# A graph kernel: the last weight's turning moved from the second aggregation into node tiles 4 to 7 of the first linear

## The reference

```python
def sage(h, W_self, W_neigh, b):           # mean over incoming edges
    agg = segment_sum(h[src], dst, num_segments=N)
    return h @ W_self + (agg * deg_inv[:, None]) @ W_neigh + b

h = relu(sage(x, W_self0, W_neigh0, b0))
x = layernorm(x + sage(h, W_self1, W_neigh1, b1))
# second layer, self loops added, norm = deg^-1/2 of both ends
g = einsum('nd,od->no', x, W) + b          # W is used turned: W[o, d]
out = segment_sum(norm[:, None] * g[col], row, num_segments=N)
x = layernorm(x + out)
```

## Time and profile before

| | |
|---|---|
| median of 3 runs | 849.19 us (848.74 to 851.98) |
| the profiled execution's own time | 849.59 us |
| its span, first to last instruction | 847.9 us |
| PE busy | 830.6 us (98%) |
| PEld, DVE, ACT, POOL busy | 83%, 54%, 21%, 54% |
| DMA | 180.52 MB, mean 213 GB/s |

### The profile page before, as it was taken

One profiled execution on the slowest core, in us unless ns is written; L12 is line 12 of the kernel. 1 busy time (PEld: TensorE's weight loads), 2 busy tenths in 40 slices (PEclk: granted clock), 3 DMA queues, 4 the chain that ended last, 5 costly groups with the idle time before them and its releaser, 6 DMA issues.

```text
span 847.9 us, 11000 instructions
## 1 busy us (share of the span) xinstructions
PE 830.6 (98%) x4295; PEld 707.9 (83%) x4295; DVE 461.3 (54%) x714; ACT 177.4 (21%) x218; POOL 459.1 (54%) x343
## 2 busy tenths in 40 slices
PE   8999999999999999999999999999999999999996
PEld 6888888888897899788888888778889889988885
DVE  6465568200017565897544677775556435455555
ACT  4111132110111113353123112222222122200000
POOL 5028887787777887885888788788620000000000
PEclk9999999999999999999999999999999999999999
DMA  9977965463776425668876668267877649555551
GB/s 332 380 304 267 350 193 168 125 176 75 213 236 180 122 57 133 249 237 286 298 282 222 243 220 284 62 176 214 240 245 255 223 150 295 189 199 199 198 193 46
DMA packets 99480, 180.52 MB, mean 213 GB/s; under 512 B 15474, under 2 KB 75898, under 8 KB 94048
## 3 DMA queue, kind: packets, MB, share of 16 engines
q1 hardware_dynamic: 60144, 124.17, 44.0%
q10 hardware_dynamic: 26896, 40.65, 13.3%
q0 software_dynamic: 12384, 14.95, 7.6%
HBM read 107.08 MB, written 72.43 MB: 212 GB/s over the span
## 4 chain that ended last, share of the span: by engine, by line
PE 61%; POOL 15%; DMA 9%; issue 8%; DVE 5%; SPq 1%; ACT 1%; POOLq 0%; ACTq 0%; DVEq 0%
PE ps L1572 19%; POOL adj_in L643 14%; PE ps L1429 12%; PE ps L1606 10%; PE ps L1589 9%; PE ps L1515 8%; DMA adj_in<-u 4%; DMA first_rows<-in_L_gnn_W_neigh 1%; DMA spare<-in_x 1%; DMA xin<-s0t_scr 1%; PE ps L1413 1%; DVE u L914 1%; PE ps L1380 1%; SPq L514 1%; DVE sacc L1303 0%
## 5 line engine op out<-in xcount | busy, mean ns | idle before, releaser
L643 POOL DMA_INDIRECT adj_out<-loops,idx_out x160 | 245.2, 1533 | 65.4 <-issue 65.4
L643 POOL DMA_INDIRECT adj_in<-mult,idx_in x160 | 198.1, 1238 | 86.8 <-issue 86.8
L1572 PE MATMUL ps<-u 128*128 128x512 f32 x840 | 190.7, 389 | 1.4 <-DVE u L914 1.4
L1572 PEld LDWEIGHTS ps<-u 128*128 128x128 f32 x840 | 157.6, 188 | 34.2 <-issue 1.6
L1484 PE MATMUL ps<-wx 128*128 128x512 f32 (+1 forms) x576 | 109.4, 351 | 1.3 <-ACT outb L761 1.3
L1484 PEld LDWEIGHTS ps<-wx 128*128 128x128 f32 x576 | 93.9, 189 | 16.9 <-ACT outb L761 1.9
L1429 PE MATMUL ps<-u 128*128 128x512 f32 x432 | 98.2, 389 | 0.0
L1515 PE MATMUL ps<-wx,u 128*128 128x256 f32 (+5 forms) x640 | 94.8, 309 | 1.2 <-DVE ht L1191 1.2
L1589 PE MATMUL ps<-u,panel_tiles 128*128 128x512 f32 (+1 forms) x400 | 93.9, 393 | 1.9 <-DVE u L914 1.9
L1429 PEld LDWEIGHTS ps<-u 128*128 128x128 f32 x432 | 81.0, 188 | 16.8
L1515 PEld LDWEIGHTS ps<-wx,u 128*128 128x128 f32 (+1 forms) x640 | 86.6, 191 | 8.2 <-DVE ht L1191 1.6
(11 more groups left out here) (167 smaller groups left out, 779.8 us busy)
## 6 DMA issues: line engine op xcount, KB each, us to landing
left_scr<-u SPq DMA_DIRECT2D x7, 2560.0 KB, 9.5
u<-left_scr SPq DMA_DIRECT2D x7, 2560.0 KB, 9.6
xt_scr<-wx ACTq DMA_DIRECT2D x10, 1024.0 KB, 9.9
u<-xt_scr SPq DMA_DIRECT2D x10, 1024.0 KB, 5.1
wx<-xt_scr SPq DMA_DIRECT2D x16, 512.0 KB, 4.0
adj_in<-u POOLq DMA_DIRECT2D x4, 1600.0 KB, 25.3
adj_out<-u POOLq DMA_DIRECT2D x4, 1600.0 KB, 16.1
wx<-adj_in SPq DMA_DIRECT2D x5, 1280.0 KB, 7.1
```

The source lines that it names most:

```text
L643: pool.indirect_dma_start(table, bass.IndirectOffsetOnAxis(ap=index[0:EP, j:j + 1], axis=0), counts[0:EP, j:j + 1], None, bounds_check=CEL ...
L1572: ins = nc.tensor.matmul(ps[:, product_bank(g, i, p), :], left_op[n % 2][:, p, k, left, :], right_op[n % 2][:, k, right, :], start=(not on ...
```

## The change

The eight rows of W are turned in node tiles 4 to 7 of the first linear, two in each, after steps 10 and 18. SP loads row k into `raw[k % 2]`, two rows behind each of the loads of x for tiles 5 to 8; from row 2 on it waits for the turning of row k-2. ACT copies the turned row into `outb[k % 2]` and stores it (`keep_turned`); from row 2 on it waits for the landing of the store of row k-2. In ACT's program this stands after `turn_hi(t + 1)` and before `evict_hi(N0, t)`. The first four rows of W_self0 are loaded when these places are free. In the second aggregation the loads, transposes, copies and stores are gone, and so are the waits for them behind it. The transposes write the same fourth bank pair.

```diff
@@ sync
             for t in range(2, NT):
                 load_x(t)
+                if t in (5, 6, 7, 8):
+                    for k in (2 * t - 10, 2 * t - 9):
+                        sp.wait_ge(w_lo_done, KD * S0)
+                        if k >= 2:
+                            sp.wait_ge(wt_turned, k - 1)
+                        sp.dma_start(raw[:, k % 2, :], w_gcn[k * P:(k + 1) * P, :]).then_inc(wt_in[k % 2], 16)
             for k in range(4):
-                sp.wait_ge(w_lo_done, KD * S0)
+                if k < 2:
+                    sp.wait_ge(wt_turned, 7 + k)
+                else:
+                    sp.wait_ge(wt_stored[k % 2], 16 * KD // 2)
                 load_w(S0, k)
@@ sync, second aggregation
-                if t < 2 or t >= 4:
-                    k = t if t < 2 else t - 2
-                    if t < 2:
-                        sp.wait_ge(right_lo, 12)
-                    else:
-                        sp.wait_ge(wt_stored[k % 2], 16 * (k // 2))
-                    sp.dma_start(late[:, k % 2, :], w_gcn[k * P:(k + 1) * P, :]).then_inc(wt_in[k % 2], 16)
...
-            for s in range(2):
-                sp.wait_ge(wt_stored[s], 16 * KD // 2)
@@ scalar
+            def keep_turned(k):
+                act.wait_ge(wt_turned, k + 1)
+                if k >= 2:
+                    act.wait_ge(wt_stored[k % 2], 16 * (k // 2))
+                else:
+                    act.wait_ge(w_lo_done, KD * S0)
+                nc.scalar.activation(outb[:, k % 2, :], pair_bank(3), ACT.Copy).then_inc(wt_copied, 1)
+                act.wait_ge(wt_copied, k + 1)
+                act.dma_start(wt_scr.rearrange("(k p) o -> p k o", p=P)[:, :, k * P:(k + 1) * P],
+                              outb[:, k % 2, :].rearrange("p (k o) -> p k o", k=KD)).then_inc(wt_stored[k % 2], 16)
...
                     turn_hi(t + 1)
+                    if t in WEIGHT_TILES:
+                        keep_turned(2 * t - 8)
+                        keep_turned(2 * t - 7)
                     evict_hi(N0, t)
@@ tensor
             def turn_weights(c):
                 pe.wait_ge(wt_in[c % 2], 16 * (c // 2 + 1))
                 if c == 0:
-                    pe.wait_ge(*summed(1, 6, 2))
+                    pe.wait_ge(flag_ready, 1)
+                    pe.wait_ge(b0c_ready, 1)
                 else:
                     pe.wait_ge(wt_copied, c)
                 for k in range(KD):
-                    ins = nc.tensor.transpose(pair_bank(3)[:, k * P:(k + 1) * P], late[:, c % 2, k * P:(k + 1) * P], ident[:, :])
+                    ins = nc.tensor.transpose(pair_bank(3)[:, k * P:(k + 1) * P], raw[:, c % 2, k * P:(k + 1) * P], ident[:, :])
                 ins.then_inc(wt_turned, 1)
@@ tensor, linear
+                    if q == N0 and t in WEIGHT_TILES and i in (10, 18):
+                        turn_weights(2 * t - 8 + (i == 18))
@@ tensor, mean1 and gather
-                        if 1 <= t <= KD:
-                            turn_weights(t - 1)
...
-                        pe.wait_ge(wt_copied, KD)
```

More of the change, by code:

```diff
@@ L56, in build @@
     SHARED = 5
+    WEIGHT_TILES = (4, 5, 6, 7)
     N0, S0, GCN = range(3)
```

## The result

The changed kernel takes 860.28 us (median of 4 runs, 859.71 to 865.68) against 849.98 for the one before beside it: ratio 1.0135, interval 1.0104 to 1.0166. The direction was right, and so was the mechanism that the forecast named, as far as it went; the size, +6.6, was too small: measured were +10.3 on the medians, and +10.1 between the two profiled executions (859.71 and 849.59, spans 858.0 and 847.9). Against the median of 849.19 that the forecast started from, the ratio makes 860.7: above its own range (852.5 to 859.5) and just above the range for 8 in 10 (845.8 to 860.5).

A forecast was written before the change was run, and what follows sets the result against it. TensorE's executed work was taken to set the time unless something makes it wait. Terms 6.8 - 8.3 - 1.2 + 7.4 + 1.9 = +6.6 gave 855.8 us against the median; own range 852.5 to 859.5, 8-in-10 range 845.8 to 860.5.

The forecast's parts named there:

- Step 1: First linear, tiles 4 to 7: the 8 groups of transposes add TensorE work, +6.8 us (bounds 6.5 to 7.1).
- Step 2: Second aggregation: without the transpose groups and the wait for ACT it gives back 8.3 us (bounds -7.0 to -8.5).
- Rival D: Second aggregation: VectorE's chain sets its time, so only 1.1 us goes; 862 us, chance 0.05.
- Step 3: First aggregation: TensorE arrives later, the scatter is done, and its wait for VectorE goes, -1.2 us (bounds -1.2 and 0).
- Step 4: First linear, tile 6: row 5's turning waits for row 2's store, starved beside the clearing, +7.4 us (bounds 0 and 11).
- rival A: First linear: queue turns go by bytes, the store isn't starved and no wait arises; 846.5 us, chance 0.27.
- Step 5: After the gap in the first linear: TensorE's clock falls to its lower level for nine matmuls, +1.9 us (bounds 0 and 3).
- Step 6: The rest: ACT's copies, later loads of x and the second weight's rows are covered by TensorE's work, 0 each.
- B: Second aggregation's end: where rival A holds, GpSimd's last scatter bounds the third stage's start; 847 to 850 us, chance 0.07.
- C: First linear, tile 7: x's store behind two weight stores causes a second wait of 3 to 5 us; 860 us, chance 0.11.

The follow-up runs named there:

- 4 KB kernel: The changed kernel with each turned row stored in 128 runs of 4 KB instead of 1024 of 512 B: 849.46 us, ratio 0.9998.
- three places: The changed kernel with a small free table as third place for turned rows, so row 4's copy waits for row 1's store: 858.89 us.

## Why the prediction was right in direction and too small

**Step 1, the transposes in the first linear: +6.8, measured +7.3.** The steps are 13.60 against 11.77, 0.91 for each of the 8 groups where I had 0.85; 0.2 above the step's upper bound of 7.1. The earlier trace rows gave 0.82 for a group and the earlier trace rows 0.85 to 0.88; I had taken a value between them. What makes a group dearer here was not tried.

**Step 2, the second aggregation: -8.3, measured -8.2.** Right: 400 matmuls in 92.07 us without a gap, and the same in all kernels without the turning there. Rival D is out.

**Step 3, the first aggregation: -1.2, measured -1.5.** The wait for VectorE of the earlier trace rows is in no profile of the changed kernel. That it goes because TensorE comes 7 us or more later is not shown: with the turning left out TensorE comes 2.2 us later (239.6 against 237.4) and the stage takes 103.72 all the same.

**Step 4, the new wait: +7.4, measured +11.3. This is the step that failed, as a term of the sum that was mis-sized.** Place, row, releaser and reason were as told: row 5 in tile 6, ACT's copy, the store of row 2, one packet for each queue in turn. The counts bear out the reason: by 98 us, when the large packets were all but through, some 24 packets of this store had gone on each engine (390 of 1024), where 23 were forecast. Three sizes were off. The clearing's first packet went at 77.3 instead of 76.5, and it was through near 98 instead of 96.8. "The rest go fast" was wrong: for the remaining 634 packets I had taken the speed of a store alone, with 1.7 us, while the queue moved only these in each microsecond from 98 to 102:
```profile
q10 hardware_dynamic: 56, 0.03, 10.0%
...
q10 hardware_dynamic: 115, 0.06, 26.9%
...
q10 hardware_dynamic: 134, 0.07, 79.2%
...
q10 hardware_dynamic: 255, 0.13, 92.6%
```
That is 560 packets in 4 us; the queue's 1024th packet since the issue went at about 102.2. Two things slowed it. In the first two of these microseconds SP's loads had 56% and 50% of the engines' time: they had been held back by the same turns as the store, and were still queued. The forecast had named this as its upper bound ("at 104, if loads share the tail": 11). In the next two the store's queue had 79% and 93% of the time itself and still moved only 134 and 255 packets, 95 and 58 ns for each, where a packet took 27 ns beside the clearing and 28 alone. Why they took longer is open, and that the upper bound comes so near is luck in this part. The third size is the 1.5 us to the semaphore, which no run shows: the first store of the kernel before, alone, landed 0.3 us after its last packet. Instead row 2's store landed 2.6 us after its queue's 1024th packet, at 104.8, when the queue had moved some 1800. So by then a good part of row 3's store, which stands behind it, was through. I read this as some of the 16 engines being ahead of others, with the landing waiting for the last; the records name no engine. The landing was 4.8 us later than forecast in all (1.2 + 2.5 + 1.1); the wait grew by 3.9, since row 5 was due 0.8 later too.

The step also lacked a second cause of the same gap, ACT's standing issue. In the changed kernel it ends 2.6 us before the landing and so hides behind it; with a third place it is alone and costs 9.5. A remedy built on the forecast's mechanism would have been the third place, and would have taken 1.8 us from the 11.3.

The Trainium skill ("DMA: Bandwidth & Descriptors", Queues, rings and completion order) has an engine drain a whole packet, typically 9 to 17 descriptors, from one ring before it turns to the next. If a record of the trace is one descriptor, the trace does not agree. Its single records alternate: of the 321 of the store from 84 to 96 us (27 ns each) 289 are followed, some 23 ns after their start, by one of 12.8 KB (479 ns), and at the end of 255 of the 289 large ones in this time one of 4 KB begins (159 ns). They are matched by time alone. The equal counts of 321, 318 and 321, at mean sizes from 0.5 to 11.5 KB, speak against turns by bytes, but would not by themselves exclude turns of many packets. The prediction's step from that page to rival A was not sound: if the store went in five turns, the clearing's turns between them would be as many packets of 12.8 KB.

**Step 5, the clock: +1.9, measured +1.6.** The windows from 103 to 111 us (start:end, length, then each engine's busy time; the last three numbers are granted clock, DMA share, GB/s):
```profile
103.00:105.00 2.00, 0.00 (x0) 0.00 (x0) 1.69 (x2) 0.44 (x2) 1.70 (x2) 0.50 1.00 217
105.00:107.00 2.00, 0.99 (x5) 1.02 (x6) 1.93 (x3) 0.86 (x1) 1.70 (x2) 0.50 1.03 276
107.00:109.00 2.00, 2.00 (x8) 1.74 (x7) 1.90 (x6) 1.02 (x1) 1.39 (x3) 0.50 0.93 237
109.00:111.00 2.00, 2.00 (x10) 1.65 (x9) 0.38 (x3) 0.01 (x1) 1.70 (x2) 0.98 0.87 208
```
The clock is at 0.50 from 103 to 109, at 0.98 after; it had fallen within the gap (0.96 from 97 to 99, 0.50 from 99 to 101). That is the lower of the two levels that the Trainium skill ("TensorE: Matmul & The Clock Gate", Part 1) gives, 1.2 GHz; the trace agrees, in the middle of a kernel too. In the experiments with a gap the slow stretch cost 1.5 to 2.7 us.

**Step 6, the rest: 0, measured +0.35** up to tile 5, which is no part of the change: with the turning in its old place or left out this stretch takes 58.83 to 59.48, and in the second profile of the changed kernel 58.61. ACT's copies of 1.0 us hold nobody up where the stores are small, as the kernel with an eighth of them shows; the issue behind them did. That loads of x issued 17 us before their turn are in time was wrong as a rule: in the 4 KB kernel that of tile 8 was issued at 83.66, needed 20.4 us, and TensorE waited 1.6 for it. In the changed kernel it needed 17.2, and the gap hid it. A term that the sum did not have at all is the wait at the end of the products, -1.7.

**The rivals.** A would have been the result if turns went by bytes; its number, 846.5, is near the 847.25 of the kernel with an eighth of the stores, which is what A amounts to, a kernel whose stores cost nothing. B did not arise: TensorE has no wait before the gather. C did not arise as told: there is no second wait in tile 7. Its time, 860, was met by another way.

The sum with measured terms: 7.3 - 8.2 - 1.5 + 11.3 + 1.6 + 0.35 = +10.85; with the -1.8 of the products and the +1.1 of the self part it is the +10.15 of the table. The 0.35 and the 1.1 are no part of the change; the 1.7 of the products are.

## What to carry to other kernels

Before a transfer is moved, count its packets, not its bytes: beside large packets of other queues it got one turn for each of theirs here, and 512 KB in 1024 packets took 26 us where it takes 3.3 alone. Lay the scratch tensor out so that the store is in long runs and pay with short ones where it is read, if that stage has DMA time to spare; here this gave the whole loss back and no more (849.46 against 849.82). When a starved transfer is estimated, take the end of what starves it as the start of its tail, let the tail share with everything that is still queued, allow for engines that lag behind the mean, and look at what the engine that issues it has to do next.

## What the runs showed of the hardware that was not expected

An issue of a DMA is not always short. With two stores of 1024 packets undrained in ACT's queue, the next issue there stood 17.37 us (after), 17.21 (three places), 16.80 (the changed kernel again) and 16.10 (smaller packets for the clearing); 12.86 where the stores of rows 0 and 1 were the undrained ones. With 512 packets a store it took 0.34, with 128 0.33. Everything behind it in ACT's program stood too. I read this as a limit on what can be outstanding in one queue. The changed kernel's trace narrows it, with the same issue in the next two tiles:
```profile
111.31 2.87 ACTq L701 DMA_DIRECT2D xt_scr<-wx  x1
...
124.90 0.35 ACTq L701 DMA_DIRECT2D xt_scr<-wx  x1
```
Counted from the records, some 1280 packets of stores were left in the queue at the first and some 1020 at the second; with some 1150 left the issue took 0.85 (smaller packets for the clearing, 124.65). So it begins to stand somewhere between these, 1020 and 1150. When it ends is less plain: between some 460 and 1240 packets were left then in the five long ones. Whether packets are what it counts was not tried.

The queues' turns came out equal to 1 or 2% in windows of 12 us, whatever the sizes: 321, 318, 321 at 11.5, 3.7 and 0.5 KB, and 271, 267, 271 at 11.3, 3.8 and 3.7 KB. Where the clearing's packets were halved the loads fell behind (412 beside 522 and 511), but only from 86 to 88 us (60 beside 87 and 87) and from 94 to 96 (36 beside 119 and 119), just before or as a load landed, where SP's queue had little left; from 88 to 94 the counts were 242, 244 and 244.
